# Transposed one-hots written to memory once and fetched again; attention rows of 65 floats in two buffers

## The chip, the core and the metric

The kernel runs on one core of a Trainium2 chip. Five engines share the core's on-chip memory: TensorE (PE, with its weight loads as PEld), VectorE (DVE), ScalarE (ACT), GpSimd (POOL) and SyncE (SP). The metric is the time on the device, in microseconds (us); lower is better.

## What is computed

A graph has 12500 nodes of 64 channels and 200000 edges, sorted by their target `dst`. Two convolution layers come first, then two attention layers. Every layer gathers a row of the source node for each edge and adds a message into the row of the target node:

```python
# convolution layer (twice): i = dst, j = src
z = concat([x[i], x[j]])
m = sigmoid(z @ Wf + bf) * softplus(z @ Ws + bs)
x = relu(x + segment_sum(m, i))
# attention layer (twice), self loops included
xl = x @ W
alpha = leaky_relu(a_src[src] + a_dst[dst] + a_edge, 0.2)
ex = exp(alpha - segment_max(alpha, dst)[dst])
out = segment_sum(xl[src] * (ex / segment_sum(ex, dst)[dst])[:, None], dst)
x = batch_norm(out + bias)            # relu after the first
```

Residual sums with layer norms stand behind the pair of convolution layers and behind the pair of attention layers.

## The kernel before

**Tiling.** Nodes lie in 98 blocks of 128. Edges are cut into 1664 steps of at most 128 edges, and all edges of a step belong to one block. Four steps are a group (416 groups), four groups are one pass of a loop (16 steps, 104 passes), 32 groups are a batch of 128 steps (13 batches). A step's one-hot is a 128 x 128 matrix with a one where an edge meets its target node. It sums messages per node on PE, and its transpose spreads a node value to the edges. Everything around the change is software pipelined by hand: `stages` writes down, for each engine, which group's work stands at which place of the loop, and semaphores join the engines.

**Gathers.** POOL issues one indirect DMA per step (`L606` in a convolution layer, `L976` in an attention layer). It fetches 128 rows of 128 floats (512 bytes) by the source indices. So there are 1664 gathers in each of the four edge stages. A completion is signalled to the other engines by a semaphore, also PE's.

**Convolution edge stage (`cg_edges`).** Per group: DVE builds four one-hots (L525) once the sum of four groups earlier is done; PE transposes them (`transposes`, L699) into a PSUM bank; ACT copies the bank to `onehot_t` (`copy_t`, L665); PE adds the gathered rows (L708) and the products of transposed one-hots and table rows (L711) into a PSUM bank (`form`); ACT and DVE compute the two nonlinearities (L671 to L683, L630 to L638); PE sums per node (`segment_sum`, L719); DVE adds into the accumulator (L648). PE's order is transposes of group u, form of u-1, sum of u-3. POOL has a ring of four groups for gathered rows: it waits for `s_X`, the end of `form`, before it writes a slot again.

**Attention edge stage (`gat_edges`).** A batch first runs a chain of small steps for the softmax weights ("the turn" in what follows): it needs all 128 gathers of the batch and, for every edge, two node values of its target. These are spread by PE with transposed one-hots in bfloat16: DVE builds the one-hots (`spread`, L525 with output `big`), PE transposes them (L1165), ACT copies them (L1119), PE multiplies (`expand`, L1173). For batch 0 that happens in `spread_first`; for the others it is woven into the loop `sums` of the batch before. In `sums` ACT weighs gathered rows (`weigh`, L1146 and L1148), DVE builds one-hots again in float32, PE sums per node (L1216), DVE accumulates (L1096, which waits for the sum). The gathered rows lie in one buffer `buf` of 128 slots, so POOL gathers group g of a batch only when `weigh` is done with group g of the batch before (`e_m`).

## Time and profile before

| | us |
|---|---|
| median of 3 runs | 12443.34 |
| lowest, highest | 12418.31, 12456.87 |
| the profiled execution, its own time | 12385.3 |
| its span | 12383.6 |
| PE, DVE, ACT busy | 6073.3, 4537.0, 3853.0 |
| POOL busy | 6568.8 |
| granted PE clock, mean | 0.646 of full speed |

The span falls into setup, two convolution edge stages, two attention edge stages, and short table and finishing stages between. POOL issues indirect gathers through all four edge stages. Spans on PE are modelled from the instruction; what waits for a PE result shows when its completion was seen.

### The profile page before, as it was taken

The page shows a single profiled execution, that of the slowest core. Times are in us where ns is not written, and L with a number is a line of the kernel's source. Part 1 is how long each engine was busy: PE and PEld are TensorE (multiplying, and loading weights), DVE is VectorE, ACT ScalarE, POOL GpSimd, SP SyncE. Part 2 cuts the span into 40 slices and gives each one's busy share as a digit, 9 for nine tenths or more (in the row PEclk, how much of TensorE's full clock was granted, in tenths as well). Part 3 has the DMA queues.
Part 4 walks back from the last instruction along what each step waited for, and adds up shares of the span by engine and source line. Part 5 has one row for each costly group of instructions (what it writes and reads, how often), then busy time and mean ns, then how long its engine had stood idle before and what let it go on. Part 6 is the DMA issues. An engine that isn't in the chain of part 4 may idle for free. (4 is left out here: it accounts for less than half of the span.)

```text
span 12383.6 us, 150453 instructions
## 1 busy us (share of the span) xinstructions
PE 6073.3 (49%) x33515; PEld 4947.5 (40%) x33516; DVE 4537.0 (37%) x13059; ACT 3853.0 (31%) x9857; POOL 6568.8 (53%) x6800
## 2 busy tenths in 40 slices
PE   2666666666666666666523333333342333343333
PEld 1444444444444555554413333333332333333332
DVE  5333333333333333333423333333352333333336
ACT  1444434444344444444312222222221222222222
POOL 1555555555455555555355555555515555555551
PEclk6888887887788888878655555555555555555555
DMA  4111111111111111111211111111101111111111
GB/s 117 37 37 38 37 37 37 37 37 37 51 39 38 40 40 39 40 40 39 53 39 39 36 40 38 38 39 36 40 22 39 39 37 38 38 39 40 36 39 31
DMA packets 325714, 498.77 MB, mean 40 GB/s; under 512 B 177366, under 2 KB 214986, under 8 KB 323979
## 3 DMA queue, kind: packets, MB, share of 16 engines
q0 software_dynamic: 214032, 440.06, 13.6%
q1 hardware_dynamic: 106316, 43.62, 1.5%
q10 hardware_dynamic: 5193, 13.44, 0.3%
q14 instruction: 144, 1.18, 0.0%
q8 instruction: 29, 0.48, 0.0%
HBM read 464.28 MB, written 32.36 MB: 40 GB/s over the span
## 5 line engine op out<-in xcount | busy, mean ns | idle before, releaser
L976 POOL DMA_INDIRECT big<-xl_table,idx_stage x3328 | 3268.5, 982 | 2395.2 <-ACT msg L1148 1334.4
L606 POOL DMA_INDIRECT big<-q_table,idx_stage x3328 | 3256.1, 978 | 2400.4 <-PE bank L711 1367.7
L1216 PE MATMUL bank<-msg,onehot 128*128 128x66 f32 x6656 | 1623.5, 426 | 1571.3 <-issue 730.2
L525 DVE TENSOR_TENSOR onehot<-iota,dst_rel 128x512 f32<-128x512 f32 x1664 | 1146.6, 689 | 3020.2 <-remote 1504.1
L1216 PEld LDWEIGHTS bank<-msg,onehot 128*128 128x128 f32 x6656 | 1488.8, 329 | 1732.1 <-issue 984.8
L1096 DVE TENSOR_TENSOR wide<-wide,bank 128x66 f32 x3328 | 732.6, 220 | 3412.2 <-remote 2554.7
L1119 ACT ACTIVATE onehot_t<-bank 128x512 bf16<-128x512 bf16 x832 | 493.8, 594 | 3854.7 <-remote 3196.3
L699 PE MATMUL bank<-ident,onehot 128*128 128x128 f32 x3328 | 697.7, 346 | 2023.2 <-DVE onehot L525 1814.8
L711 PEld LDWEIGHTS bank<-big,onehot_t 128*128 128x128 f32 x6656 | 1176.3, 248 | 621.5 <-issue 621.5
L699 PEld LDWEIGHTS bank<-ident,onehot 128*128 128x128 f32 x3328 | 447.2, 171 | 2139.3 <-DVE onehot L525 1212.3
L708 PE MATMUL bank<-big,ident 128*128 128x512 f32 x1664 | 1248.7, 843 | 26.0 <-DMA big<-q_table,idx_stage 12.4
L711 PE MATMUL bank<-big,onehot_t 128*128 x6656 | 1143.4, 329 | 0.0
L665 ACT ACTIVATE onehot_t<-bank 128x512 f32<-128x512 f32 x832 | 495.6, 596 | 2081.2 <-PE bank L699 1210.1
L1165 PE MATMUL bank<-ident_bf,big 128*128 128x128 bf16 x3328 | 497.2, 305 | 1241.3 <-DVE big L525 981.3
L719 PE MATMUL bank<-msg,onehot 128*128 128x67 f32 (+1 forms) x6656 | 955.8, 294 | 21.4 <-issue 15.3
L719 PEld LDWEIGHTS bank<-msg,onehot 128*128 128x128 f32 x6656 | 949.3, 220 | 23.4 <-issue 16.5
L1148 ACT ACTIVATE msg<-big,work 128x64 f32 (+1 forms) x3328 | 878.6, 337 | 0.1
L648 DVE TENSOR_TENSOR wide<-wide,bank 128x67 f32 (+1 forms) x3328 | 734.9, 221 | 357.8 <-PE bank L719 1.9
L671 ACT ACTIVATE work<-bank 128x512 f32<-128x512 f32 x832 | 496.5, 597 | 1168.3 <-PE bank L711 783.2
L1165 PEld LDWEIGHTS bank<-ident_bf,big 128*128 128x128 bf16 x3328 | 291.9, 130 | 1276.4 <-DVE big L525 1007.0
L525 DVE TENSOR_TENSOR big<-iota,dst_rel 128x512 bf16<-128x512 f32 x832 | 576.1, 694 | 352.8 <-remote 246.0
L676 ACT ACTIVATE work<-work 128x512 f32<-128x512 f32 x832 | 523.9, 630 | 103.4
(214 smaller groups left out, 4591.3 us busy)
## 6 DMA issues: line engine op xcount, KB each, us to landing
big<-q_table,idx_stage POOLq DMA_INDIRECT x3328
big<-xl_table,idx_stage POOLq DMA_INDIRECT x3328
big<-in_edge_attr ACTq DMA_DIRECT2D x12, 1024.0 KB, 4.7
q_table<-wide SPq DMA_DIRECT2D x12, 1024.0 KB, 5.1
xl_table<-big SPq DMA_DIRECT2D x12, 520.0 KB, 4.6
edge_rows<-big SPq DMA_DIRECT2D x1, 3341.0 KB, 11.6
x_dram<-big SPq DMA_DIRECT2D x1, 3136.0 KB, 16.1
out<-big SPq DMA_DIRECT2D x1, 3104.0 KB
```

What stands on the lines that cost most here:

```text
L525: return nc.vector.tensor_tensor(to, k.iota[:, :].unsqueeze(1).broadcast_to([P, GROUP, P]), k.dst_rel[:, ds(s, GROUP)].unsqueeze(2).broadc ...
L606: pool.indirect_dma_start(out=ring[:, u, s % GROUP, :], out_offset=None, in_=k.q_table, in_offset=bass.IndirectOffsetOnAxis(ap=k.idx_stage ...
L648: nc.vector.tensor_tensor(to, to, k.psum[4 + c % 2][:, i * P:i * P + width], ALU.add).then_inc(s_add if i < GROUP - 1 else s_acc, 1)
L699: last_one = nc.tensor.transpose(k.psum[c % 2][:, i * P:(i + 1) * P], k.onehot[:, c % UNROLL, i, :], k.ident[:, :])
L708: nc.tensor.matmul(k.psum[2 + j][:, :], k.ident[:, :], ring[:, slot].rearrange("p i c -> p (i c)"), start=True, stop=False)
L711: last_one = nc.tensor.matmul(k.psum[2 + j][:, i * P:(i + 1) * P], k.onehot_t[:, j, i, :], p_tab[:, ds(at[i], 2 * C)], start=False, stop=i ...
L719: last_one = nc.tensor.matmul(k.psum[4 + c % 2][:, i * P:i * P + width], k.onehot[:, c % UNROLL, i, :], k.msg[:, c % UNROLL, i, 0:width], ...
L976: pool.indirect_dma_start(out=buf[:, s, :], out_offset=None, in_=k.xl_table, in_offset=bass.IndirectOffsetOnAxis(ap=k.idx_stage[:, s:s + 1 ...
L1096: nc.vector.tensor_tensor(to, to, k.psum[6 + c % 2][:, i * P:i * P + C + 2], ALU.add).then_inc(e_add if i < GROUP - 1 else e_acc, 1)
L1148: last_one = nc.scalar.activation(k.msg[:, c, i, 0:C], flat(gather[:, ds(s + i, 1), 0:C]), ACT.Copy, scale=flat(wsw[:, ds(s + i, 1), 0:1]))
L1165: last_one = nc.tensor.transpose(turned_bank[c % 2][:, i, :], a_onehot[:, c, i, :], k.ident_bf[:, :])
L1216: last_one = nc.tensor.matmul(k.psum[6 + c % 2][:, i * P:i * P + C + 2], k.onehot[:, c % UNROLL, i, :], k.msg[:, c % UNROLL, i, 0:C + 2], ...
```

## The change

- In the first convolution edge stage ACT copies every transposed bank a second time, to bfloat16 (`copy_bf`, last in ACT's list of a stage), into one of two slots of two groups each. SP stores a full slot to a new table `turned` (256 KB each, two per pass). PE's transposes wait for this copy where they waited for `copy_t`.
- In the second convolution edge stage there are no transposes on PE. SP fetches the slots back, and `copy_t` reads them.
- In both attention edge stages the one-hots for the spread, their transposes and ACT's copies are gone, from `spread_first` too. SP fetches slots, each after `a_X`, the completion of `expand`, has freed it, and `expand` reads the slot directly. `expand` moves from two groups behind to one.
- The table of attention rows has 65 floats per row (260 bytes) in place of 128, and its filling with zeros is gone. The gathered rows have two buffers of 128 slots; POOL waits for `weigh` of the same group two batches back.

Cut to its core:

```diff
-TW = 2 * C
+TW = C + 1
@@ cg_edges, SP
+            def keep(it):
+                for h in range(2):
+                    sp.wait_ge(s_Tb, it * UNROLL + 2 * h + 2)
+                    sp.sem_inc(s_turn, 1)
+                    sp.dma_start(turned_rows(k, it, h), slots[h].rearrange("p g i c -> p (g i c)")).then_inc(s_hold[h], 16)
+            def fetch(it):
+                for h in range(2):
+                    wait(sp, s_Tc, (it - 1) * UNROLL + 2 * h + 2 if not isinstance(it, int) or it else 0)
+                    sp.sem_inc(s_turn, 1)
+                    sp.dma_start(slots[h].rearrange("p g i c -> p (g i c)"), turned_rows(k, it, h)).then_inc(s_hold[h], 16)
+            move = keep if layer == 0 else fetch
@@ cg_edges, ACT
+                def copy_bf(c):
+                    if layer == 0:
+                        if c % 2 == 0:
+                            wait(act, s_hold[c // 2], it * 16)
+                        nc.scalar.activation(slots[c // 2][:, c % 2, :, :], k.psum[c % 2][:, :].rearrange("p (i c) -> p i c", c=P),
+                                             ACT.Copy).then_inc(s_Tb, 1)
-                    stages(u, first, last, (0, copy_t), (2, sigmoids), (1, logs))
+                    stages(u, first, last, (0, copy_t), (2, sigmoids), (1, logs), (0, copy_bf))
@@ cg_edges, PE
                 def transposes(c):
+                    if layer == 1:
+                        return
                     wait(pe, s_S, n[c + 1])
-                    wait(pe, s_Tc, n[c - 1])
+                    wait(pe, s_Tb, n[c - 1])
@@ gat_edges
-    buf = k.big[:, 0:P * TW].rearrange("p (s c) -> p s c", c=TW)
+    buf = [k.big[:, i * P * TW:(i + 1) * P * TW].rearrange("p (s c) -> p s c", c=TW) for i in range(2)]
@@ gat_edges, SP
+            def fetch(it):
+                for h in range(2):
+                    wait(sp, a_X, (it - 1) * UNROLL + 2 * h + 2 if not isinstance(it, int) or it else 0)
+                    sp.sem_inc(s_turn, 1)
+                    sp.dma_start(slots[h].rearrange("p g i c -> p (g i c)"), turned_rows(k, it, h)).then_inc(s_held[h], 16)
@@ gat_edges, POOL
-                        wait(pool, e_m, (b - 1) * BGROUPS + (s // GROUP + 1))
+                        wait(pool, e_m, (b - 2) * BGROUPS + (s // GROUP + 1))
@@ gat_edges, PE
+            def expand(it, step, column, c):
+                at = load_offsets(k, pe, SPREAD_ROW, step + c * GROUP, GROUP, 2 * PARTS)
+                if c % 2 == 0:
+                    pe.wait_ge(s_held[c // 2], it * 16 + 16)
-                            stages(u, first, last, (2, lambda c: expand(spread_sems[1], n, (b * BIT + it) * ITER + P, column, c)),
-                                   (0, lambda c: transposes(spread_sems[1], n, c)))
+                            stages(u, first, last, (1, lambda c: expand((b + 1) * BIT + it, (b * BIT + it) * ITER + P, column, c)))
```

PE in the loop `sums` of an attention stage, before: the spread products of one group (L1173, a row of registers ahead of each), the transposes of a later group (L1165), and then the sum per node of the next (L1216) and its load of offsets:

```order
440 L1173 MATMUL bank<-spread_bf,onehot_t 128x6
441 L1173 ISA
442 L1173 MATMUL bank<-spread_bf,onehot_t 128x6
443 L1173 ISA
444 L1173 MATMUL bank<-spread_bf,onehot_t 128x6
445 L1173 ISA
446 L1173 MATMUL bank<-spread_bf,onehot_t 128x6
447 L64 REGISTER_ALU
448 L1165 MATMUL bank<-ident_bf,big 128x128 x4
449 L1216 MATMUL bank<-msg,onehot 128x66 x4
450 L531 ISA
451 L531 TENSOR_LOAD offsets
```

The same place of the changed kernel, from one group's sum (L1225) to the next one's, with the spread products (L1185) between:

```order
363 L1225 MATMUL bank<-msg,onehot 128x66 x4
364 L531 TENSOR_LOAD offsets
365 L1185 ISA
366 L1185 MATMUL bank<-spread_bf,big 128x6
367 L1185 ISA
368 L1185 MATMUL bank<-spread_bf,big 128x6
369 L1185 ISA
370 L1185 MATMUL bank<-spread_bf,big 128x6
371 L1185 ISA
372 L1185 MATMUL bank<-spread_bf,big 128x6
373 L1225 MATMUL bank<-msg,onehot 128x66 x4
```

The transposes are gone, and the products read `big` (a fetched slot) in place of `onehot_t`.

ACT in the loop of the first convolution edge stage, one group, before (L665 the copy of the transposes, L683 to L676 the nonlinearities):

```order
107 L665 ACTIVATE onehot_t<-bank 128x512
108 L682 ISA
109 L682 ACTIVATE msg<-ae 128x4x2
110 L683 ACTIVATE work<-work 128x4x64
111 L64 REGISTER_ALU
112 L671 ACTIVATE work<-bank 128x512
113 L673 ACTIVATE work<-work 128x512
114 L675 ISA
115 L676 ACTIVATE work<-work 128x512
```

The same of the changed kernel:

```order
112 L699 ACTIVATE onehot_t<-bank 128x512
113 L723 ISA
114 L723 ACTIVATE msg<-ae 128x4x2
115 L724 ACTIVATE work<-work 128x4x64
116 L65 REGISTER_ALU
117 L712 ACTIVATE work<-bank 128x512
118 L714 ACTIVATE work<-work 128x512
119 L716 ISA
120 L717 ACTIVATE work<-work 128x512
121 L705 ACTIVATE wide<-bank 128x512
```

The second copy of the bank (L705) comes last in the group.

## Rows read from the trace of the kernel before

**Rows 1.** Busy time by stretch: length, PE, PEld, DVE, ACT, POOL, clock, DMA share, GB/s

```profile
377.50:3230.00 2852.50, 1784.10 (x8914) 1379.36 (x8913) 1034.58 (x3250) 1153.76 (x2428) 1576.35 (x1629) 0.81 0.14 37
3294.50:6064.00 2769.50, 1822.21 (x9116) 1403.50 (x9116) 1048.37 (x3323) 1142.30 (x2073) 1618.16 (x1679) 0.81 0.15 39
6189.90:9154.00 2964.10, 1117.01 (x6851) 989.98 (x6851) 985.29 (x3047) 708.69 (x2549) 1643.82 (x1690) 0.50 0.14 37
9279.60:12247.00 2967.40, 1115.82 (x6851) 989.07 (x6851) 984.79 (x3046) 704.45 (x2549) 1637.43 (x1690) 0.50 0.14 37
```

**Rows 2.** Costliest groups: count, busy us, mean ns, idle before and its releaser

```profile
L606 POOL DMA_INDIRECT big<-q_table,idx_stage x3328 | 3256.1, 978 | 2400.4 <-PE bank L711 1367.7
L665 ACT ACTIVATE onehot_t<-bank 128x512 f32<-128x512 f32 x832 | 495.6, 596 | 2081.2 <-PE bank L699 1210.1
```

**Rows 3.** Timeline, first attention stage, while POOL gathers batch 0 (start, length)

```profile
6265.68 0.60 ACT L1119 ACTIVATE onehot_t<-bank 128x512 bf16<-128x512 bf16 x1 [21.79 <-issue]
6266.45 0.64 PE L1173 MATMUL bank<-spread_bf,onehot_t 128*128 x4 [21.16 <-issue]
...
6267.03 0.61 PE L1165 MATMUL bank<-ident_bf,big 128*128 128x128 bf16 x4
6267.99 0.94 POOL L976 DMA_INDIRECT big<-xl_table,idx_stage  x1 [0.30 <-issue]
...
6288.11 0.60 ACT L1119 ACTIVATE onehot_t<-bank 128x512 bf16<-128x512 bf16 x1 [21.83 <-remote]
```

**Rows 4.** The same loop 100 us later; POOL's last gather of batch 0 began at 6349.26

```profile
6349.26 0.94 POOL L976 DMA_INDIRECT big<-xl_table,idx_stage  x1 [0.30 <-issue]
...
6371.90 0.61 PE L1165 MATMUL bank<-ident_bf,big 128*128 128x128 bf16 x4
6372.55 0.60 ACT L1119 ACTIVATE onehot_t<-bank 128x512 bf16<-128x512 bf16 x1 [0.59 <-PE bank L1165]
```

**Rows 5.** Timeline of POOL and ACT around the turn between batches 1 and 2

```profile
6814.86 0.94 POOL L976 DMA_INDIRECT big<-xl_table,idx_stage  x1 [0.30 <-issue]
6820.33 0.94 POOL L976 DMA_INDIRECT big<-xl_table,idx_stage  x1 [4.53 <-ACT msg L1148]
...
6823.74 1.05 ACT L1148 ACTIVATE msg<-big,work 128x64 f32 x4
...
6857.32 1.05 ACT L1148 ACTIVATE msg<-big,work 128x64 f32<-128x64 f32 x4
```

**Rows 6.** First gather, ACT's turn copy of batches 0 and 12, last accumulation

```profile
6189.91 0.96 POOL L976 DMA_INDIRECT big<-xl_table,idx_stage  x1 [0.79 <-POOL idx_stage L978]
...
6401.76 0.49 ACT L1131 ACTIVATE work<-bank 128x384 f32<-128x384 f32 x1 [6.07 <-PE bank L1189]
...
9064.90 0.49 ACT L1131 ACTIVATE work<-bank 128x384 f32<-128x384 f32 x1 [15.25 <-PE bank L1189]
...
9152.08 1.32 DVE L1096 TENSOR_TENSOR wide<-wide,bank 128x66 f32 x4 [0.46 <-PE bank L1216]
```

**Rows 7.** Timeline, last batch (no gathers, no spread): two groups' sums on PE

```profile
9086.97 1.78 PEld L1216 LDWEIGHTS bank<-msg,onehot 128*128 128x128 f32 x8 [0.62 <-issue]
...
9089.27 1.78 PEld L1216 LDWEIGHTS bank<-msg,onehot 128*128 128x128 f32 x8 [0.52 <-issue]
```

**Rows 8.** Timeline, second convolution edge stage, from one sum over the next group's work

```profile
3999.07 1.00 PE L719 MATMUL bank<-msg,onehot 128*128 128x64 f32 x8
...
4004.04 0.77 DVE L525 TENSOR_TENSOR onehot<-iota,dst_rel 128x512 f32<-128x512 f32 x1 [5.03 <-remote]
...
4004.86 1.11 PE L699 MATMUL bank<-ident,onehot 128*128 128x128 f32 x4 [4.79 <-DVE onehot L525]
4005.77 1.91 PE L708 MATMUL bank<-big,ident 128*128 128x512 f32 x2
4007.47 1.77 PE L711 MATMUL bank<-big,onehot_t 128*128 x8
```

**Rows 9.** DMA issues: line engine op xcount, KB each, median us to landing

```profile
q_table<-wide SPq DMA_DIRECT2D x12, 1024.0 KB, 5.1
```

More of the change, by code:

```diff
@@ L41 @@
 BGROUPS = P // GROUP
+ITERS = GROUPS // UNROLL
 CH = NBATCH
@@ L567, in cg_edges @@
     s_row, row_base = k.rows, list(k.row_base)
-    k.row_base = [r + GROUPS // UNROLL * GROUP * 16 for r in row_base]
-    s_turn, s_blank = k.sem(n + "turn"), k.sem(n + "blank")
+    k.row_base = [r + ITERS * GROUP * 16 for r in row_base]
+    s_turn = k.sem(n + "turn")
+    s_Tb, s_hold = k.sem(n + "trans_bf"), [k.sem(f"{n}hold{h}") for h in range(2)]
+    slots = turned_slots(k.wide[:, 0:2 * GROUP * P])
     p_tab = k.big[:, 0:NB * 2 * C]
@@ L902, in gat_edges @@
     s_turn = k.sem(n + "turn")
-    spread_sems = [[k.sem(f"{n}first{x}") for x in range(4)], [a_S, a_T, a_Tc, a_X]]
+    s_held = [k.sem(f"{n}held{h}") for h in range(2)]
     acc = k.wide[:, NB * C:NB * (C + AW)]
-    buf = k.big[:, 0:P * TW].rearrange("p (s c) -> p s c", c=TW)
+    buf = [k.big[:, i * P * TW:(i + 1) * P * TW].rearrange("p (s c) -> p s c", c=TW) for i in range(2)]
     w = k.work
@@ L953, in _ @@
             k.clear_old(sp)
+            def fetch(it):
+                for h in range(2):
+                    wait(sp, a_X, (it - 1) * UNROLL + 2 * h + 2 if not isinstance(it, int) or it else 0)
+                    sp.sem_inc(s_turn, 1)
+                    sp.dma_start(slots[h].rearrange("p g i c -> p (g i c)"), turned_rows(k, it, h)).then_inc(s_held[h], 16)
+            fetch(0)
+            with sp.Fori(1, ITERS) as it:
+                fetch(it)
         @block.gpsimd
@@ L992, in _ @@
             v.wait_ge(s_zero, 2)
-            def spread(sems, n, step, c):
-                made, turned = sems[0:2]
-                wait(v, turned, n[c - 3])
-                build_onehot(nc, k, a_onehot[:, c], step + c * GROUP).then_inc(made, 1)
-            def spread_first(it, first, last):
-                n = counts(v, it * UNROLL, -3, 0)
-                for u in range(UNROLL):
-                    stages(u, first, last, (0, lambda c: spread(spread_sems[0], n, it * ITER, c)))
-            pipelined(v, BIT, spread_first)
             def batch(b, p, turn):
                 first_group = b * BGROUPS
-                gather = buf
+                gather = buf[p]
                 link = Chain(v, s_ch, b * LINKS)
@@ L1101, in sums @@
                         stages(u, first, last, (2, begin))
-                        if not ends(b):
-                            stages(u, first, last, (0, lambda c: spread(spread_sems[1], n, step + P, c)))
                         stages(u, first, last, (2, lambda c: add(c, 1)), (0, onehot), (2, lambda c: add(c, 2)), (2, lambda c: add(c, 3)))
@@ L1113, in _ @@
             act.preload_act_table_set("natural_log_exp_and_others")
-            def spread(sems, n, c):
-                turned, copied, used = sems[1:4]
-                wait(act, turned, n[c + 1])
-                wait(act, used, n[c - 1])
-                nc.scalar.activation(onehot_t[:, c % 2, :, :], turned_bank[c % 2], ACT.Copy).then_inc(copied, 1)
-            def spread_first(it, first, last):
-                n = counts(act, it * UNROLL, -1, 4)
-                for u in range(UNROLL):
-                    stages(u, first, last, (0, lambda c: spread(spread_sems[0], n, c)))
-            pipelined(act, BIT, spread_first)
             def batch(b, p, turn):
                 first_group = b * BGROUPS
-                gather = buf
+                gather = buf[p]
                 act.wait_ge(s_x3, b + 1)
@@ L1152, in sums @@
                         stages(u, first, last, (0, weigh))
-                        if not ends(b):
-                            stages(u, first, last, (0, lambda c: spread(spread_sems[1], n, c)))
                 pipelined(act, BIT, sums)
```

70 lines of the change are left out of this document (31 added, 39 removed).

## The prediction

> **What bounds the kernel now.** I began with busy time by stretch [rows 1]. No engine is full in any of the four edge stages: POOL is busy 1576 of 2852 us in the first and 1644 of 2964 us in the third, and no other engine exceeds two thirds. The stages take 11,553 of the 12,384 us, so something between the engines sets their pace. The second view is the costliest groups [rows 2]: POOL's gather costs 978 ns and is preceded by 2400 us of idle time over 3328 gathers, mostly waits for the end of a form (L711); ACT's copy waits 2081 us, mostly for the transposes (L699). Both wait for PE, which is not busy enough to explain it.
>
> The timeline gives the answer. While POOL gathers without pause in the first attention stage, one gather per 1.25 us (0.94 and 0.30 us idle ahead), PE's transposes are drawn at 6267.03 and last 0.61 us, and ACT's copy of them starts at 6288.11, with a wait of 21.83 us that no engine is named for [rows 3]. From copy to copy are 22.4 us, with two completions of PE in them, so about 11 us each. After POOL's last gather the same copy follows the same transposes at once [rows 4]. The same mark of a wait stands in the second convolution stage: DVE's one-hot starts at 4004.04 after a wait of 5.03 us, though the sum that it waits for is drawn as over at 4000.07, four us before [rows 8]. I read this so: **PE's completions are seen late while POOL gathers, and catch up when POOL pauses.** The Trainium skill ("Perfetto Trace Analysis", Tensor Engine Instruction) says that the profiler's end of a TensorE instruction is an estimate; so a part of the lateness could be work that ends later than drawn. The short gap of [rows 4], on identical instructions, speaks against that for most of it.
>
> Each chain through PE thus costs work plus lateness, and lateness shrinks only when POOL stops. That makes a balance: POOL's floor is 16 x 1.25 = 20.0 us per pass (by the mean of 978 ns and 0.30, 20.5), and the second convolution stage takes 2769.5 / 104 = 26.6 us. In attention the period of a batch is (9064.90 - 6401.76) / 12 = 221.9 us [rows 6], where POOL needs 128 x 1.25 = 160. Of it the turn, from the last weigh of one batch to the first of the next, takes 6857.32 - 6824.79 = 32.5 us, with POOL idle from shortly after its gather of 6820.33 [rows 5]; the sums take 189.4, 5.92 per group. Without gathers and spread the sums need 2.3 us per group on PE [rows 7].
>
> **First convolution stage.** Added are 416 copies on ACT of 596 ns each as the present copy [rows 2], 248 us. ACT is busy 1154 of 2852 us [rows 1], and its copies wait for PE, so the new copy, last in ACT's group, stands mostly where ACT would wait for the next transposes. PE's transposes now wait for it two groups back instead of for the first copy. The 208 stores of 256 KB leave the engines' DMA share of 0.14 [rows 1] nearly as it is: a whole table of 1024 KB lands in 5.1 us [rows 9], the slot has about 13 us until ACT needs it again. Bounds: nothing if all is in waits (below nothing has no mechanism, no work goes), +248 if every copy delays the next. I take +60, a quarter, near the lower end because ACT is idle 60% of the time.
>
> **Second convolution stage.** Removed: 1.11 us of transposes per group on PE [rows 8], their completion, and the dependence of form on the one-hot. The chain of [rows 8] is sum (1.00), lateness, one-hot (0.77), transposes (1.11), form (1.91 and 1.77, overlapping to 3.5). ACT's copy stays, but from a slot that SP has fetched ahead; SP waits for `s_Tc`, an ACT completion, never late, and the fetch has two groups, 13 us, for a transfer bounded by 5.1 us [rows 9]. With only the transposes off the path a pass is 26.6 - 4 x 1.11 = 22.2 us; with the one-hot off too, 19.1, under POOL's 20.5, which then binds. With neither (POOL waits for form, and form for its bank, with unchanged lateness) it is 26.6. I take 22.2, since PE sits between two completions in each group whichever chain leads: 104 x 4.4 = **-460**. Bounds: 0 and -104 x 6.1 = -634. One thing can go below zero: PE's granted clock. It is 0.81 here with PE busy 66% of the stage, and 0.50 (1.2 GHz) in attention with 38% [rows 1]. After, PE is busy (1822 - 416 x 1.11) / (104 x 22.2) = 59%, far nearer to the first, so I keep 0.81. At 0.71 the 4.5 us of form and sum become 5.1, +0.6 x 416 = +250; that stands in the range.
>
> **Attention, the period.** Per group PE loses 0.61 us of transposes [rows 3], ACT a copy of 0.60, DVE a bfloat16 one-hot, and one of three PE completions goes. The turn, 32.5 us, is PE's and DVE's small steps and doesn't change. The gain is at least nothing, and 32 x 0.61 = 20 us if PE's time is all on the path: 221.9 to 202. I take the middle, **212**. Were completions no longer the limit, sums could fall to POOL's 5.0 per group, not below without POOL's gathers running into the turn: 160 + 32.5 = 193. The second buffer gives POOL nothing in the steady state: it still gathers group g when `weigh` is done with some group g, two batches back instead of one, at the same pace. POOL is never waited for at the turn any more; before it trailed by one group at most [rows 5].
>
> **Attention, the ends.** Here the second buffer does act. At the start POOL gathers 256 slots without pause, 256 x 1.25 = 320 us, before it must wait for `weigh`. Batch 0's spread has 32 completions of expand, and at some 11 us each [rows 3] they would need 350; SP's fetches wait for them. So the spread ends when POOL pauses, and ACT's turn copy comes at about 320 us in place of 211.9 (6401.76 - 6189.91, [rows 6]); the lower bound is 212 if completions of a lone chain are not late. At the end, sums of the last but one batch have no gathers beside them: 32 x 2.3 + 32.5 = 106 us. The tail after the last turn copy is 9153.40 - 9064.90 = 88.5. A layer is 320 + 11 x 212 + 106 + 88.5 = 2847 us, against 211.9 + 12 x 221.9 + 88.5 = 2963: -117, and **-234** for both. Bounds: with P at 221.9 a layer is 2955, -16 in all; with P at 193 and a start of 212 it is 2530, -868 in all; what makes it slower is the second rival.
>
> In the loop each slot is fetched after `a_X` of its second group and read again three groups later, 17.8 us at 5.92. The fetch costs under 5.1 us [rows 9], the lateness 4 [rows 8] to 11 us [rows 3]: 9 to 16 us, so it just fits. For the transfer the Trainium skill ("DMA: Bandwidth & Descriptors", Anatomy of one DMA) gives a fit for the software path of 2.0 us plus bytes / 436e3, so an estimate of 2.6 us for a slot; by it the slack is 2.5 us larger and the sum the same, with less for the second rival. The gathers of 260 bytes move half as much as those of 512. Their share of the DMA engines is part of 0.14 [rows 1], so even doubled it would fill no engine. The same page (Specifications) names 512 bytes as the least for line rate, with a read-modify-write below; the trace of before has no shorter rows, and by that rule the fetches and gathers land later, which is the first thing that could use up the slack just worked out, and adds to the chance of the second rival.
>
> **Sum.** 60 - 460 - 234 = -634. The profiled execution took 12385.3 us, 1.7 more than its span, so 11,751; the median of the runs is 1.0047 times it, so **about 11,800**. The forecast's own range, with the bounds partly together, is 11,400 to 12,350.
>
> **Rivals.** *First, the lateness goes.* If it came from the rows' transfers, half the bytes would relieve it; fewer completions might also let the queue drain. Then attention runs at POOL's pace: 212 + 11 x 193 + 106 + 88.5 = 2530 a layer, -868 for both; the second convolution stage at 20.5 a pass, -634; the first +60: -1442, so 10,943 x 1.0047 = 11,000. If gathers also run on through the turn, a layer is 2080 + 32.5 + 74 = 2190, and the whole 10,300. For it: PE is busy under two thirds everywhere. Against: lateness in [rows 3] follows POOL's pauses and not the bytes, the DMA engines being nearly idle.
>
> *Second, slower: expand waits for the fetch.* PE reads a slot that SP refills only after seeing `a_X`. PE's queue is in order, so behind a waiting expand stands the sum of the next group, behind that DVE's accumulation and one-hot, then `weigh` and POOL. It decides when lateness plus fetch exceeds 17.8 us. Were `a_X` seen behind another completion of PE, as two stand in the 22.4 us of [rows 3], it would be 22 + 5 = 27; 5 us of wait per pass of four groups is the middle between none and that. A period has 8 passes: 212 + 40 = 252, for 2 x 11 periods +880, so +246 in all: 12,631 x 1.0047 = 12,690. Against: while PE waits, POOL gets no new `weigh`, pauses, and the lateness ends.
>
> *Third, nothing moves.* The second convolution stage stays bound by POOL's waits for form (1367.7 us of idle time before the gather end with L711, [rows 2]), the period stays 221.9, and the ends cancel: +60 - 16 = +44, so 12,490. That the change doesn't do what it says I see no room for: in three stages the transposes are gone from PE's list.
>
> **How the numbers follow.** Forecast 0.55, first rival 0.20, second 0.15, third 0.10. About 0.3% (37 us) is what a measurement of this kernel can tell from no change. Faster by more than that: 0.55 + 0.20 = 0.75; within it: 0.07 out of the third; slower: 0.15 and the rest of the third, 0.18. The range takes the forecast and the third whole, half of the second and the nearer half of the first: 10,950 to 12,650.
>
> **What would show it.** Second convolution stage: 22 us a pass, no L699, and idle time before the gather shrunk; at 26 the transposes were not on the path. First: 27.4 to 28.8 us a pass. Attention: first turn copy at 320 us, periods of 212 and one of 106 at the end. If periods are near 193 with waits of DVE for POOL's rows, the first rival; if PE idles before L1185, released by SP's queue, the second. Waits without a name on ACT and DVE must still be there while POOL gathers; if gone, my reading of the lateness is wrong, or it hangs on the rows' length.

## The result and the profile after

| | us |
|---|---|
| changed kernel, median of 5 runs (lowest, highest) | 12551.94 (12508.35, 12586.0) |
| kernel before, median of 5 runs | 12445.24 |
| ratio, 95% interval | 1.0062, 1.0033 to 1.009 |
| profiled execution of the changed kernel: time, span | 12553.0, 12550.9 |

The changed kernel is 0.6% slower. I had forecast 11,800, 5% faster; the time lies inside my range of 10,950 to 12,650, but the sign is wrong. The first view to read is again busy time by stretch (length; PE, PEld, DVE, ACT, POOL; clock; DMA share; GB/s), against [rows 1]. The attention stretches here reach from the first gather to the last accumulation:

```profile
377.50:3500.00 3122.50, 1753.71 (x8782) 1355.62 (x8782) 1015.39 (x3194) 1319.14 (x2793) 1535.20 (x1620) 0.79 0.16 50
3650.00:6150.00 2500.00, 1598.40 (x7301) 1255.05 (x7300) 1027.57 (x3243) 1126.09 (x2028) 1579.55 (x1649) 0.77 0.22 64
6310.70:9295.00 2984.30, 918.43 (x5187) 861.06 (x5187) 764.89 (x2629) 506.76 (x2132) 1604.54 (x1690) 0.50 0.16 37
9424.00:12414.00 2990.00, 918.26 (x5187) 861.02 (x5187) 764.81 (x2629) 507.69 (x2132) 1608.84 (x1690) 0.50 0.16 37
```

Engines lost work as planned (PE 1117 to 918 us in an attention stage, ACT 709 to 507), and the stages did not follow. Of the costliest groups, POOL's gather of the convolution stages, ACT's copy of the turned bank and the second copy (count, busy, mean ns, idle before) answer to [rows 2]:

```profile
L634 POOL DMA_INDIRECT big<-q_table,idx_stage x3328 | 3206.5, 963 | 2538.1 <-PE bank L754 1331.1 <-issue 931.3 <-remote 274.1
...
L699 ACT ACTIVATE onehot_t<-bank 128x512 f32<-128x512 f32 x416 | 247.8, 596 | 1134.9 <-PE bank L742 1043.5 <-remote 46.1 <-issue 43.4
L705 ACT ACTIVATE wide<-bank 128x512 bf16<-128x512 f32 x416 | 240.9, 579 | 0.0
```

POOL is idle longer than before (2400), and its waits for form are what they were. The second copy costs ACT 241 us, near the 248 that I had worked out, and ACT is never idle just before it (0.0). From the first to the last accumulation, or in attention from the first gather, the stages took:

| us | before | after | forecast | measured |
|---|---|---|---|---|
| first convolution stage | 2905 | 3223 | +60 | +318 |
| second | 2745 | 2544 | -460 | -201 |
| both attention stages | 5930 | 5975 | -234 | +45 |

The changes come to +162, the span's to +167. ACT's turn copy gives the inside of an attention stage, as in [rows 6]: the first gather, then batches 0, 1, 11 and 12, and the last accumulation:

```profile
6310.32 0.97 POOL L1026 DMA_INDIRECT big<-xl_table,idx_stage  x1 [0.80 <-POOL idx_stage L1028]
...
6622.78 0.49 ACT L1152 ACTIVATE work<-bank 128x384 f32<-128x384 f32 x1 [312.23 <-remote]
...
6882.48 0.49 ACT L1152 ACTIVATE work<-bank 128x384 f32<-128x384 f32 x1 [28.07 <-PE bank L1198]
...
9110.08 0.49 ACT L1152 ACTIVATE work<-bank 128x384 f32<-128x384 f32 x1 [17.35 <-PE bank L1198]
...
9205.99 0.49 ACT L1152 ACTIVATE work<-bank 128x384 f32<-128x384 f32 x1 [17.38 <-PE bank L1198]
...
9293.55 1.32 DVE L1132 TENSOR_TENSOR wide<-wide,bank 128x66 f32 x4 [0.46 <-DVE wide L1132]
```

The first copy comes after 312 us (forecast 320), the last period is 96 us (106), the tail 89. But ten periods between batch 1 and batch 11 are (9110.08 - 6882.48) / 10 = 222.8 us each, where I had 212 and the kernel before 221.9; the first one is 260.

**One pass of an attention stage.** The timeline of the changed kernel, first stage, from the first weigh of a batch, shows why:

```profile
7340.54 0.95 POOL L1026 DMA_INDIRECT big<-xl_table,idx_stage  x1 [27.35 <-ACT msg L1169]
...
7343.68 1.94 PE L1225 MATMUL bank<-msg,onehot 128*128 128x66 f32 x8
...
7345.00 0.59 DVE L1132 TENSOR_TENSOR wide<-wide,bank 128x66 f32 x2 [1.47 <-PE bank L1225]
...
7346.82 1.97 PE L1225 MATMUL bank<-msg,onehot 128*128 128x66 f32 x8 [1.12 <-issue]
...
7348.59 0.29 PE L1185 MATMUL bank<-spread_bf,big 128*128 x4
...
7369.31 0.94 POOL L1026 DMA_INDIRECT big<-xl_table,idx_stage  x1 [0.30 <-issue]
7372.70 0.59 DVE L1132 TENSOR_TENSOR wide<-wide,bank 128x66 f32 x2 [25.93 <-remote]
...
7374.69 0.95 POOL L1026 DMA_INDIRECT big<-xl_table,idx_stage  x1 [4.44 <-ACT msg L1169]
...
7379.30 0.59 DVE L1132 TENSOR_TENSOR wide<-wide,bank 128x66 f32 x2 [4.83 <-remote]
```

The batch's second sum is accumulated at 7345.00. Its third is drawn as over at 7345.62 (7343.68 + 1.94), and the accumulation that waits for it starts at 7372.70, 27 us later and 3.4 us after the start of POOL's last gather of the run (24 of them here, where the batch begins). The fourth sum, over at 7348.8, is accumulated only at 7379.30. ACT waits for the same completion before it can weigh, and only then does POOL get new slots. So a pass of 16 gathers is a **run of POOL plus a gap**: with some 30 us for the turn, (222.8 - 30) / 8 = 24.1 us are 16 x 1.25 = 20 and 4. Of POOL's 99 runs in the stage 67 have 16 gathers. What PE, DVE and ACT do inside the run is hidden, spread and transposes among it, in the kernel before too.

**The second convolution stage** repeats it with runs of 8 (the ring's four groups, two freed at a time):

```profile
3704.22 1.05 PE L754 MATMUL bank<-big,onehot_t 128*128 x8
3704.46 0.94 POOL L634 DMA_INDIRECT big<-q_table,idx_stage  x1 [0.30 <-issue]
3707.18 0.60 ACT L712 ACTIVATE work<-bank 128x512 f32<-128x512 f32 x1 [5.75 <-remote]
...
3707.93 0.97 POOL L634 DMA_INDIRECT big<-q_table,idx_stage  x1 [2.52 <-remote]
```

The last gather of a run starts at 3704.46, form's completion is seen 2.7 us later, the next run starts at 3707.93. From the first to the last start of a run are 7 x 1.25 = 8.75 us, and 3.47 to the next: 12.2, twice in a pass, 24.4. The stage's 2544 us over 104 passes are 24.5.

**The first convolution stage.** The sum is drawn as over at 2044.91, the one-hot that waits for it starts 6.2 us later; between them are POOL's gathers, of which the last is shown. In [rows 8], from the second stage, these were 4 us. Behind the one-hot stand transposes and form, and behind these POOL's next run, so the whole of it is in the pass. POOL's pauses of over 1 us add up to 844 us in this stage before and 1171 after, 327 more, which is the stage's 318:

```profile
2043.90 1.01 PE L762 MATMUL bank<-msg,onehot 128*128 128x67 f32 x8
...
2049.07 0.95 POOL L634 DMA_INDIRECT big<-q_table,idx_stage  x1 [0.30 <-issue]
2051.13 0.69 DVE L525 TENSOR_TENSOR onehot<-iota,dst_rel 128x512 f32<-128x512 f32 x1 [7.12 <-remote]
```

### The profile page after: what moved, and what is told of

Its sections match the earlier page's. It is cut to its first block and busy times, and to the rows that moved or that the text cites. A ratio compares the mean times of both kernels' runs of the same rounds, so it can differ in the third digit from the quotient of the medians.

```text
span 12550.9 us, 141049 instructions
## 1 busy us (share of the span) xinstructions
PE 5479.2 (44%) x28523; PEld 4564.4 (36%) x28524; DVE 4105.6 (33%) x12227; ACT 3653.1 (29%) x9441; POOL 6460.4 (51%) x6799
## 3 DMA queue, kind: packets, MB, share of 16 engines
q14 instruction: 136, 1.11, 0.0%
## 5 line engine op out<-in xcount | busy, mean ns | idle before, releaser
L1026 POOL DMA_INDIRECT big<-xl_table,idx_stage x3328 | 3201.3, 962 | 2366.8 <-ACT msg L1169 1250.7
L1225 PE MATMUL bank<-msg,onehot 128*128 128x66 f32 x6656 | 1623.2, 426 | 3098.1 <-DVE wide L1132 1874.0
L1225 PEld LDWEIGHTS bank<-msg,onehot 128*128 128x128 f32 x6656 | 1481.7, 328 | 3165.3 <-ACT msg L1169 1878.1
L762 PE MATMUL bank<-msg,onehot 128*128 128x67 f32 (+1 forms) x6656 | 1069.1, 315 | 941.0 <-issue 816.0
L762 PEld LDWEIGHTS bank<-msg,onehot 128*128 128x128 f32 x6656 | 1034.0, 237 | 986.9 <-issue 895.5
L1167 ACT ACTIVATE msg<-work 128x8 f32 (+1 forms) x832 | 174.4, 210 | 3565.0 <-remote 3131.2
L742 PE MATMUL bank<-ident,onehot 128*128 128x128 f32 x1664 | 361.5, 355 | 1415.6 <-DVE onehot L525 1266.7
L676 DVE TENSOR_TENSOR wide<-wide,bank 128x67 f32 (+1 forms) x3328 | 737.6, 222 | 357.7 <-PE bank L762 1.7
L742 PEld LDWEIGHTS bank<-ident,onehot 128*128 128x128 f32 x1664 | 232.0, 176 | 1473.0 <-DVE onehot L525 753.7
L699 ACT ACTIVATE onehot_t<-bank 128x512 f32<-128x512 f32 x416 | 247.8, 596 | 1134.9 <-PE bank L742 1043.5
L717 ACT ACTIVATE work<-work 128x512 f32<-128x512 f32 x832 | 523.9, 630 | 103.4
L1185 PEld LDWEIGHTS bank<-spread_bf,big 128*128 128x128 bf16 x3328 | 348.5, 150 | 520.1 <-issue 514.6
L714 ACT ACTIVATE work<-work 128x512 f32<-128x512 f32 x832 | 523.8, 630 | 26.7
L1185 PE MATMUL bank<-spread_bf,big 128*128 x3328 | 267.9, 179 | 505.5 <-issue 297.0
```

Of the source, the lines that this page charges most:

```text
L676: nc.vector.tensor_tensor(to, to, k.psum[4 + c % 2][:, i * P:i * P + width], ALU.add).then_inc(s_add if i < GROUP - 1 else s_acc, 1)
L742: last_one = nc.tensor.transpose(k.psum[c % 2][:, i * P:(i + 1) * P], k.onehot[:, c % UNROLL, i, :], k.ident[:, :])
L762: last_one = nc.tensor.matmul(k.psum[4 + c % 2][:, i * P:i * P + width], k.onehot[:, c % UNROLL, i, :], k.msg[:, c % UNROLL, i, 0:width], ...
L1026: pool.indirect_dma_start(out=buf[p][:, s, :], out_offset=None, in_=k.xl_table, in_offset=bass.IndirectOffsetOnAxis(ap=k.idx_stage[:, s:s ...
L1185: last_one = nc.tensor.matmul(near[:, ds(column + (c * GROUP + i) * SLOT, 2 * PARTS)], slot[:, c % 2, i, :], spread_bf[:, ds(at[i], 2 * PA ...
L1225: last_one = nc.tensor.matmul(k.psum[6 + c % 2][:, i * P:i * P + C + 2], k.onehot[:, c % UNROLL, i, :], k.msg[:, c % UNROLL, i, 0:C + 2], ...
```

## The experiments

Behind the result came five groups of runs, each on one chip, each beside runs of the kernel before; a run is named by its number (e1 to e18), and a stage's time is from its one profiled execution. To read them one must know that **the lateness of PE's completions comes and goes from one group to the next.** The kernel before took 9934 us in the first group, 12470, 11981 and 12472 in the next three, and 12440 in the last, which went to the same chip as the first. Within a group it held still (19 runs of 9922 to 9942 in the first). So comparisons stand only inside a group, and I name groups by this time. As far as the traces show, only PE's completions are late: in the trace of before DVE starts at most 0.03 us after the ACT instruction that it waited for (L630 after L676, 261 waits in the convolution stages), and PE's transposes of the first stage at most 0.14 us after DVE's one-hot (398).

**Theories.** A, alternation: a stage takes POOL's runs plus the gaps that the held completions make; work inside the runs is free, work between the held completion's being seen and POOL's next release is not. Rival B: fewer instructions and completions on PE shorten the pass. For the first convolution stage the rivals are ACT's copy, its place in the order, and SP's stores.

### Copy, place and stores

```diff
@@ ACT, e1, e9, e14 (kernel before; PE's transposes wait for s_Tb)
+    nc.scalar.activation(slots[c // 2][:, c % 2, :, :], k.psum[c % 2][:, :].rearrange("p (i c) -> p i c", c=P),
+                         ACT.Copy).then_inc(s_Tb, 1)
-    stages(u, first, last, (0, copy_t), (2, sigmoids), (1, logs))
+    stages(u, first, last, (0, copy_t), (2, sigmoids), (1, logs), (0, copy_bf))
@@ SP, in e2, e8, e15 besides
+    sp.dma_start(turned_rows(k, it, h), slots[h].rearrange("p g i c -> p (g i c)")).then_inc(s_hold[h], 16)
@@ ACT, e16
+    stages(u, first, last, (0, copy_t), (0, copy_bf), (2, sigmoids), (1, logs))
```

Expected of e1, second copy only:

> The kernel before, with ACT's second copy of each transposed bank in the first convolution stage, last in its group, and PE's transposes waiting for it; nothing is stored or fetched. From the first to the last accumulation that stage took 2905 us before and 3223 us changed. If ACT's copy and the wait for it are the cause, the stage takes about 3220 us here and the whole some 12700; if the stores of SP are the cause (PE's completions then come later), it takes under 2960 us and the whole 12390 to 12440.

Expected of e2, second copy and stores:

> The same and SP's 208 stores of 256 KB; nothing fetches them, all other stages are those of before. By either theory the stage takes 3220 us as in the changed kernel, and the whole about 12700. What it adds to the run without stores is the price of the stores: 260 us or more if they are the cause, under 60 if the copy is.

Both came in the group of 9934 us: 9934.6 and 9931.8, ratios 1.0002 (0.9992 to 1.0011) and 0.9996 (0.9986 to 1.0006). The stage took 2130 and 2131 us, 20.5 a pass, POOL's own pace. So they did not tell the two apart, but they showed what the lateness is worth. In e2 the same place with the same work:

```profile
1404.69 1.01 PE L750 MATMUL bank<-msg,onehot 128*128 128x67 f32 x8
...
1405.84 0.69 DVE L526 TENSOR_TENSOR onehot<-iota,dst_rel 128x512 f32<-128x512 f32 x1 [1.52 <-PE bank L750]
```

The one-hot starts 0.14 us after the sum's end, with an engine named for the wait.

Expected of e5, the kernel before again:

> The kernel before, unchanged, for its trace. The first comparison with other kernels showed it at 9934 us and gathers in POOL's steps of 1.25 us without pauses in the convolution stages, where the trace of before showed 12384. If the difference lies in the chip, a chip like the second one gives 9920 to 9945 us, with every completion of PE seen within 0.1 us of its drawn end; one like the first gives 12400 and completions 4 to 10 us late.

Expected of e8, second copy and stores again:

> The kernel before with ACT's second copy and SP's stores in the first convolution stage, a second time. Where completions of PE are late, that stage takes 3220 us and the whole 12700; where they are not, 2130 us and 9930 to 9945 as in the first run of it.

These fell into the group of 12470 us, one run of each. Before (e5): 12584.0, completions late again, stages of 2930 and 2889 us. Copy and stores (e8): 12850.0, first stage 3210, second 2866. The price that the first stage of the changed kernel paid is there, +280, without any other part of the change.

Expected of e9, second copy only, again:

> The kernel before with ACT's second copy alone, nothing stored. On a chip with late completions the first convolution stage takes 2905 to 2930 us without it and 3180 to 3224 with copy and stores. If the wait of the transposes for a copy that stands last in ACT's group is the cause, it takes some 3200 us without the stores too; if the stores delay PE's completions, under 2980.

In the group of 11981 us e9 took 12117.7, first stage 2785 against 2630 of the second. The difference of 155 lay between my cases, on a chip with less lateness, and without a trace of before. So the four were run in one group:

Expected of e13, the kernel before, beside e14 to e16:

> The kernel before, for its trace beside the next three. With late completions its two convolution stages do the same work but for a column and take nearly the same time, 2620 to 2930 us each, as the chip has it.

Expected of e14, second copy only:

> ACT's second copy alone, last in its group. Late chips have differed in how late they are, so the first stage is to be read against the kernel before of this same chip. If the copy is the cause, the stage is some 300 us longer than that of before and the run with stores adds nothing; if the stores are, it is at most 60 longer. On the last chip the first stage was 155 us longer than the second one, of before's form; so I expect 100 to 160, about half.

Expected of e15, second copy and stores:

> Second copy and stores. With late completions the first stage is 280 to 320 us longer than in the kernel before; the part that the run with the copy alone does not have is the price of the stores, 130 to 200 us by my guess. Without late completions nothing moves in any of these.

Expected of e16, second copy, placed first:

> The second copy alone, but right behind the first one in ACT's group instead of behind the logarithms of the group before. If what costs is that PE's transposes wait for a copy that stands behind work which itself waits for a completion of PE, the first stage is within 30 us of the kernel before. If it is the 0.58 us of ACT's time wherever it stands, or the later clearing of the bank, it stays 100 us or more longer.

| group of 12472 us | whole, ratio | first conv. stage | mean lateness of late sums, us |
|---|---|---|---|
| before (e13) | 12474.3 (one run) | 2866 | 3.77 |
| copy (e14) | 12542.5, 1.005 (1.002 to 1.0081) | 2951 | 3.98 |
| copy and stores (e15) | 12762.2, 1.0199 (1.0165 to 1.0234) | 3202 | 5.27 |
| copy, placed first (e16) | 12518.1, 1.004 (1.0015 to 1.0065) | 2916 | 4.09 |

The last column is worked out from every sum of the stage whose completion is recorded over 1 us after its drawn end: 184, 193, 199 and 193 of 416. The groups of instructions say the same. DVE's one-hot between 400 and 2700 us, in the kernel before, with the copy, and with copy and stores (count, busy, mean ns, idle time before it and its releasers):

```profile
L525 DVE TENSOR_TENSOR onehot<-iota,dst_rel 128x512 f32<-128x512 f32 x332 | 231.2, 696 | 1242.5 <-remote 638.6 <-PE bank L719 578.4 <-issue 25.5
```

```profile
L526 DVE TENSOR_TENSOR onehot<-iota,dst_rel 128x512 f32<-128x512 f32 x322 | 224.0, 696 | 1277.7 <-remote 715.8 <-PE bank L737 547.4 <-issue 14.5
```

```profile
L526 DVE TENSOR_TENSOR onehot<-iota,dst_rel 128x512 f32<-128x512 f32 x294 | 204.1, 694 | 1367.0 <-remote 855.9 <-PE bank L750 487.4 <-issue 23.7
```

The waits marked remote, in which no engine is named, are 1.92, 2.22 and 2.91 us for each one-hot. The copy costs 84 us and its place 35 of them; the second stage, the same in all four, spreads over 36 us (2809 to 2845), so 84 is about twice the scatter and 35 can't be told from it. **The stores cost 252**, clear of it; by the medians of the whole program 70, 46 with the copy first, and 220 more with the stores. The stores leave the DMA engines nearly idle (share 0.18), and ACT doesn't wait for them to land: it is never idle just before its second copy. They act through the completions: late sums are seen 1.3 us later, and 199 of these are 257 us. POOL's pauses of over 1 us add up to 792, 861, 1163 and 843 us, which is where the stage's time goes. I had guessed 130 to 200 us for the stores and 100 to 160 for the copy.

### Gathers, buffers

Expected of e3, half of the gathers:

> The changed kernel with every second gather left out in all four edge stages, so half of the rows are stale. If PE's completions are held back by POOL's runs of gathers and a pass is a run plus some 4 us, the period of an attention batch falls from 223 to 8 x (8 x 1.25 + 4) + 30 = 142 us, and the second convolution stage from 24.4 us a pass to about 15.4, where PE's own work ends it. If the lateness has another source (the number of completions, the fetches), the period stays above 200 us and the pass above 22.

Expected of e12, half of the gathers, again:

> The changed kernel with every second gather left out in all edge stages, so half of the rows are stale. With late completions: if the lateness goes with POOL's runs of gathers, the attention period falls from 223 to about 142 us, toward the 98 us of the run without late completions, and the second convolution stage from 24.6 us a pass to about 15.4; if it goes with the chip alone, whatever POOL does, they stay near 200 and 22.

```diff
@@ POOL, both gathers
+    if s % 2:
+        continue
```

In the group of 9934 us (e3, 6677.5): attention period 99 us, second convolution stage 13.0 us a pass. In that of 11981 (e12, 7720.6): period 133, second stage 13.6, first 17.6, both as without lateness or near it, and nearly all completions of the first stage's sums (372 of 387) are recorded within 0.02 us of their ends. In the attention stages A holds in the late group: 142 had been worked out as runs of 8 and gaps, 133 came, with runs mostly of 6, 8 and 12, for 220 with all gathers (e11). The second stage's 15.4 was too long, as little lateness was left there. The lateness goes with POOL's gathers, since with half of them it is gone from the first stage; yet it isn't POOL alone, as the first group had every gather and none of it. Leaving out a gather also leaves out its transfer and its signals, so these runs don't say which of the three holds PE's completions.

Expected of e4, changed kernel, one buffer:

> The changed kernel with one buffer of 128 slots for attention rows (65 floats) and POOL waiting for the weighing of the batch before, as before the change. If the second buffer only moves time between the ends, the period stays at 223 us, the first turn copy comes at 175 to 212 us instead of 312, the fast last-but-one period of 96 us is gone, and a layer takes 2960 to 2975 us against 2984. If two buffers lengthen the period (POOL's runs of 16 instead of 3 to 14), it falls to about 212 and a layer takes some 2850.

```diff
-    buf = [k.big[:, i * P * TW:(i + 1) * P * TW].rearrange("p (s c) -> p s c", c=TW) for i in range(2)]
+    buf = [k.big[:, 0:P * TW].rearrange("p (s c) -> p s c", c=TW)] * 2
-    wait(pool, e_m, (b - 2) * BGROUPS + (s // GROUP + 1))
+    wait(pool, e_m, (b - 1) * BGROUPS + (s // GROUP + 1))
```

In the group of 9934 us e4 took 9841.7, ratio 0.991 (0.9894 to 0.9927), with periods of 178 to 180 us where the kernel with only the copy (e1, before's attention) has 183, the first turn copy at 165, layers of 2412 and 2399 us for 2452 and 2450. So fetched one-hots and short rows gain where completions are on time, 3 to 4 us a batch. Its question, what the second buffer does to the period, it could not answer there.

Expected of e7, kernel before with two buffers and short rows:

> The kernel before with rows of 65 floats in two buffers of 128 slots and nothing else: transposes, their copies and the spread on DVE, ACT and PE stay. Without late completions: if the buffers bring the gain of the changed kernel, this one comes to the same 9420 us; if the removed spread is needed too (sums with the spread cannot go at POOL's 5.0 us per group and catch the turn up), it lies between 9500 and 9850. With late completions: 12385 to 12600, as the spread's completions make the start longer than in the changed kernel (32 groups at 22 us cannot end before POOL pauses at 320 us).

```diff
@@ kernel before
-TW = 2 * C
+TW = C + 1
-    wait(pool, e_m, (b - 1) * BGROUPS + (s // GROUP + 1))
+    wait(pool, e_m, (b - 2) * BGROUPS + (s // GROUP + 1))
```

In the group of 12470 us three runs of e7 took 12584 to 12659 (a fourth took 23503 us, and no cause is known), ratio 1.0108 (1.0061 to 1.0155), a little above what I expected. The first turn copy comes at 380 us, the last period is 108, those between are 225 and 224 against 223 in e5: the second buffer and short rows do nothing for the period. A layer is 3052 and 3036 us against 2983 and 2978. So of the changed kernel's parts the buffers and short rows cost 58 to 69 us a layer. The fetched one-hots (e6, layers of 2987 and 2991) give most of it back by a shorter start (316 for 380) and end. Beside e7, e6 also tests what the spread's removed work is worth in the period, with the same buffers and rows: 223 for 225 and 224.

Expected of e6, changed kernel again:

> The changed kernel, unchanged. Where completions of PE are not late, POOL is the bound of all four stages: the convolution stages stay at 20.5 us a pass, and in attention the second buffer lets POOL gather through the turn, so a layer is 1664 x 1.252 = 2083 us, and 10 + 28 + 70 behind it, 2190 against 2450: the whole about 9420 us, 5% faster. The rival: weighing gates POOL as before, since POOL is always two batches ahead; then the period stays at 180 us and the whole at 9840. On a chip with late completions it takes about 0.6% longer than the kernel before.

Expected of e17, changed kernel once more:

> The changed kernel once more. Without late completions: 20.5 us a pass in both convolution stages, and in attention either 2190 us a layer and 9420 in all (the second buffer lets POOL gather through the turn) or 9840 as with one buffer. With late completions 0.4 to 0.6% more than the kernel before.

e6 took 12525.3, ratio 1.0043 (1.0024 to 1.0062), and e17 12448.0, ratio 1.0019 (0.9998 to 1.0041), both with late completions; the second can't be told from no change. The stages repeat: 3180 and 3118, 2553 and 2536, attention 2979 to 2991 with a first period of 254 to 259 us, then 219 to 227, and a last one of 96 to 98. Against e5, the kernel before in e6's group, the convolution stages change by +250 and -336 where the result had +318 and -201, so the sizes of single stages are good to 70 to 140 us.

### Cutting the chain

```diff
@@ DVE, kernel before, both convolution stages (bfloat16, ring of four)
+    def turn(c):
+        wait(v, s_T, n[c - 3])
+        build_onehot(nc, k, early[:, c % UNROLL], it * ITER + c * GROUP).then_inc(s_E, 1)
-    stages(u, first, last, (0, onehot), (2, softs), (3, message), (4, accumulate))
+    stages(u, first, last, (0, turn), (1, onehot), (2, softs), (3, message), (4, accumulate))
@@ PE
-    nc.tensor.transpose(k.psum[c % 2][:, i * P:(i + 1) * P], k.onehot[:, c % UNROLL, i, :], k.ident[:, :])
+    nc.tensor.transpose(turned_bank[c % 2][:, i, :], early[:, c % UNROLL, i, :], k.ident_bf[:, :])
```

Expected of e10, kernel before with early one-hots:

> The kernel before with one-hots of their own for the transposes in both convolution stages, in bfloat16, built a group ahead by DVE; the one-hot for the sum comes a group later. It adds a DVE instruction and stores nothing. If the convolution stages are bound by the chain sum, one-hot, transposes, form, and the gain of the second one in the changed kernel came from cutting it and not from fewer transposes, both stages fall to 24 to 25.5 us a pass with late completions, the whole to 11900 from 12450. If PE's transposes themselves were the cost, both stay at 27 to 28 us. Without late completions both are bound by POOL at 20.5 and nothing moves (9930).

Expected of e11, changed kernel with early one-hots:

> The changed kernel with those early bfloat16 one-hots in the first convolution stage; the second copy and the stores stay. With late completions the first stage falls from 31 us a pass to 25 or 26 if the chain is what made it dear, and the whole to 11950; if the stores are, it stays above 28. Without late completions it shows the changed kernel's attention stages: 2190 us each and 9420 in all if the second buffer lets POOL run through the turn, 9840 if it does not.

Expected of e18, kernel before with early one-hots, again:

> The kernel before with early one-hots for the transposes. Without late completions POOL is the bound and it takes what the kernel before takes, within 0.2%; with them 24 to 25.5 us a pass in both convolution stages and 2 to 5% less in all.

The kernel before with early one-hots: 11729.5, ratio **0.979** (0.9772 to 0.9807), in the group of 11981 us (e10), and 11880.5, ratio **0.9558** (0.9524 to 0.9591), in that of 12440 (e18). The convolution stages take 24.1 and 24.6 us a pass, as the second one of the changed kernel, though PE still makes every transpose (in bfloat16, 0.26 us each for 0.35) and DVE makes two one-hots for one. The changed kernel with it (e11): 11735.2, 0.9795 (0.9778 to 0.9812), first stage 24.2 a pass with copy and stores inside. In this one group the first stage takes 2503 us without copy and stores and 2519 with them, and the second 2506 with transposes and 2490 without. So once no late sum stands ahead of transposes and form, copy and stores cost 16 us and the transposes 16: the stores' 252 us were the price of making later a completion that a chain waited for. POOL's row in 2300 us of the second convolution stage, in the group of 11981 us, with early one-hots (e10) and in before's form (e9):

```profile
L609 POOL DMA_INDIRECT big<-q_table,idx_stage x1515 | 1551.0, 1024 | 738.1 <-issue 420.3 <-remote 202.8 <-PE bank L718 114.9
```

```profile
L619 POOL DMA_INDIRECT big<-q_table,idx_stage x1439 | 1399.0, 972 | 883.6 <-issue 405.2 <-PE bank L729 347.6 <-remote 130.7
```

POOL issues 1515 gathers for 1439, and waits for form, named or not, 318 us for 478. This version beats both kernels where completions are late; where they are on time it was not run.

## Why the prediction was wrong

The failed step is the model "Each chain through PE thus costs work plus lateness", with the lateness kept as it was while work is taken out or put in. The traces show a pass as POOL's run plus a gap instead, so work taken out inside the run gains nothing, and what makes a completion later is paid in full. The three terms that rest on it miss by 258, 259 and 279 us, together 796 of the 802 us by which the profiled execution missed 11,751.

- **Reading the bound: right.** PE's completions late while POOL gathers, catching up in its pauses: every late trace shows it, and the traces on time show the convolution stages at POOL's 20.5 us a pass. What I could not see in one trace is that the lateness is no constant of the kernel, and that it is worth 2500 us of 12445.
- **First convolution stage: wrong, +60 for +318, outside my bound of +248.** The step that failed reads "The 208 stores of 256 KB leave the engines' DMA share of 0.14 nearly as it is". The share was about right (0.16) and was the wrong price. By e13 to e15 the stores are 252 us and the copy 84. Nothing in my list of mechanisms let a DMA of SP touch PE's completions.
- **Second convolution stage: direction right, mechanism and size wrong, -460 for -201.** The term was 4 x 1.11 us a pass of transposes, to 22.2 us. The early one-hots give the same stage with the transposes in place (2506 us for 2490), so their time was not what went; it was the wait of form for a late sum. What was left is a run of eight and its gap, twice, 24.4; I had no term for a gap after each run.
- **Attention's period: wrong, 212 for 223.** I took the middle between PE's time off the path and nothing; it is nothing, or at most 2 us of 225 (e7 against e6). The transposes stand in POOL's run. My sentence that POOL keeps "the same pace" behind `weigh` was right, and is the reason.
- **The ends: right.** 312 for 320, 96 for 106. But the first period, 260 us, in which the sums of batch 0 meet POOL at the head of a long run, was missing: 48 us a layer over my 212.
- **Second rival** (expand waits for the fetch): not what decided. In the loops of both attention stages (1528 products between 6680 and 9290 us in the first) PE is never idle just before L1185, and the passes have their 24 us from POOL's run and gap. Waits for fetches stand in the spread of batch 0. The slower outcome came by a way I had not named. **First rival**, the lateness goes: not by shorter rows (e7), but it was absent in one group, for the kernel before too.
- **Range.** That it held the time is luck: it was wide, and three misses of one sign stayed inside it. 0.18 for slower was too little for a kernel whose pace hangs on something that no engine's row shows.

PE's clock was 0.79 and 0.77 in the convolution stages for 0.81, within what I had allowed (0.71) and no cause: with early one-hots it is 0.78 and 0.77 at 24.6 us a pass (e18). My second figure for a slot's transfer took a fit for the software path, while the profile lists what SP's queue moves as hardware_dynamic; nothing rested on it. The rule of the Trainium skill ("DMA: Bandwidth & Descriptors", Specifications) on transfers under 512 bytes made no difference that a run shows: rows of 260 bytes with two buffers left the period where it was (e7).

## What to carry to other kernels

Where a producer works in runs and everything else catches up in its pauses, time is saved only in the gap from the last completion of a run to the next release; ask of each instruction on which side it stands before pricing it. Look for a buffer that a late completion frees and that early work reuses (the one-hot ring here): a second, cheap copy of that work cut 2 to 4% of the whole, and in the convolution stages as much as removing it did. And compare kernels only within one group of runs beside the kernel before: the same code took 9934 and 12440 us on the same chip.

## What the runs showed of the hardware

- PE's completions were seen within 0.02 us of their drawn ends in one group (e1, e2) and, where late, 4 us late in the mean in others, up to 27 and 30 us at the head of a batch; the kernel before took 9934 and 12440 us on the same chip. What sets this is open, also whether the work ends late or its signal travels late. Within a group fewer gathers took the lateness away from a stage and stores added to it; nothing else that a kernel did moved it much.
- The two kinds of group differ in what was recorded, too. The kernel with only the copy made the same gathers in e1 and e14, and the trace on time holds 108,435 records of DMA landings, the late one 27,134. Missing records are one way to a wait marked remote, so the readings here go by the starts of instructions. Whether the recording has a part in the lateness itself was not tested.
- In late groups the sum's completion in the first convolution stage is seen at steps after the start of POOL's run, most often at 7.2 and 8.6 us without stores (46 and 72 of 183 late sums in e13). With stores 109 of 197 come between 9.9 and 11.5 (e15), after the start of the run's last gather at 8.75; with the copy alone 29 of 192 do (e14). The steps are some 1.4 us apart and not POOL's 1.25; I have no cause for them.
- The effect of SP's stores on the completions of PE, at a DMA share of 0.18, is shown as a difference of runs (252 us, 0 on time, 16 or less with the chain cut); its mechanism is not.
- Whether the second buffer takes the turn off POOL's path where completions are on time stays open: the changed kernel itself never ran in such a group.
